# A fused graph-and-scan kernel: the first group's u projections one body sooner, and the B and C projection one step sooner

## What is computed

```
x = x + gnn(norm(x), adj)
x = x + ffn(norm(x))

gnn:  e = leaky_relu(sj + si + ab);  a = adj * exp(e);  transition = a / (rowsum(a) + 1e-12)
      H = sum over k of (Xk @ Wk[k] + bk[k]),  Xk = transition @ Xk;   relu(H)

ffn:  h = x @ W_fc1.T + b_fc1
      u, z = split(h @ W_in.T);  u = silu(causal convolution of u over 4 taps + conv_b)
      dt, B, C = split(u @ W_xproj.T)               # 32 + 16 + 16 columns
      delta = softplus(dt @ W_dt.T + b_dt)
      state[t] = exp(delta * A) * state[t-1] + (delta * u) * B[t]     # 1024 channels x 16 states
      y = sum over states of state * C + u * D;  y = y * silu(z)
      out = (y @ W_out.T) @ W_fc2.T + b_fc2
```

## Time and profile before

| | |
|---|---|
| median of 3 runs | 3723.85 us (3723.45 to 3725.98) |
| the profiled execution | 3726.6 us, its span 3724.8 us |
| instructions in the span | 43683 |
| DVE busy | 3520.6 us (95%) |
| PE busy, its weight loads | 3459.2 us (93%), 1949.2 us (52%) |
| POOL busy | 3411.5 us (92%) |
| ACT busy | 2961.1 us (79%) |
| mean granted TensorE clock | 0.988 of full speed |
| DMA | 183.68 MB, mean 49 GB/s |

### The profile page before, as it was taken

The page is one execution under the profiler, slowest core; times in us unless marked ns, Lnnn a source line. Parts: engine busy times, 40 slices in busy tenths (PEclk is TensorE's granted clock), DMA queues, the critical chain, the costliest instruction groups (busy, mean ns, idle before and its releaser), DMA issues.

```text
span 3724.8 us, 43683 instructions
## 1 busy us (share of the span) xinstructions
PE 3459.2 (93%) x11130; PEld 1949.2 (52%) x11130; DVE 3520.6 (95%) x2877; ACT 2961.1 (79%) x6578; POOL 3411.5 (92%) x1703
## 2 busy tenths in 40 slices
PE   6899999999999999999999999999999999999887
PEld 3555555555555555555555555555555555555443
DVE  0499999999999999999999999999999999999998
ACT  2588878888888888888788888888888888887774
POOL 0299999999999999999999999999999999999998
PEclk9899999999999999999999999999999999999999
DMA  3111101111101111100111110111110111110110
GB/s 112 53 56 59 59 9 53 56 58 58 59 9 53 56 59 58 58 23 39 56 58 58 59 44 18 58 56 58 58 59 9 53 56 59 58 54 9 46 51 9
DMA packets 50720, 183.68 MB, mean 49 GB/s; under 512 B 7356, under 2 KB 33220, under 8 KB 42086
## 3 DMA queue, kind: packets, MB, share of 16 engines
q1 hardware_dynamic: 48898, 174.17, 12.1%
q10 hardware_dynamic: 1636, 7.83, 0.6%
HBM read 164.15 MB, written 17.83 MB: 49 GB/s over the span
## 4 chain that ended last, share of the span: by engine, by line
POOL 56%; issue 32%; PE 5%; DVE 4%; ACT 2%; POOLq 1%; DMA 0%; SPq 0%; DVEq 0%; ACTq 0%
POOL st L425 38%; POOL st L416 10%; POOL du_sb L406 4%; POOL delta L398 3%; DVE st L967 2%; DVE st L955 1%; PE y_ps L775 1%; POOL rstd L383 1%; POOLq L192 1%; ACT dec L491 1%; PE g L926 1%; PE g L795 0%; PE dec L700 0%; DMA rows<-bk_dram 0%; PE d_ps L812 0%
## 5 line engine op out<-in xcount | busy, mean ns | idle before, releaser
L425 POOL TENSOR_TENSOR st<-st,bc 128x1024 f32<-128x1024 f32 x1024 | 2405.0, 2364 | 146.0 <-DVE st L967 146.0
L967 DVE TENSOR_TENSOR_SCAN st<-dec,st 128x1024 f32<-128x1024 f32 x1024 | 2312.6, 2274 | 23.4 <-ACT dec L491 18.5
L775 PE MATMUL y_ps<-st,ident 128*128 128x512 f32 x4096 | 1919.0, 603 | 122.6 <-POOL st L425 120.3
L491 ACT ACTIVATE dec<-delta,decay 128x254 f32<-128x254 f32 x4096 | 1691.5, 463 | 310.1 <-DVE st L967 308.1
L775 PEld LDWEIGHTS y_ps<-st,ident 128*128 128x128 f32 x4096 | 742.7, 190 | 964.9 <-issue 643.9
L955 DVE TENSOR_TENSOR st<-du,bc 128x1024 f32<-128x1024 f32 x736 | 883.8, 1201 | 22.3 <-ACT du L477 22.0
L416 POOL TENSOR_TENSOR st<-du_sb,bc 128x1024 f32<-128x1024 f32 x288 | 680.8, 2364 | 0.1
L812 PE MATMUL d_ps<-xnT,wxz 128*128 128x256 f32 x1024 | 264.5, 404 | 70.2 <-DVE u L992 69.5
L992 DVE SCALAR_TENSOR_TENSOR u<-d_ps,chan,u 128x250 f32<-128x250 f32 (+2 forms) x768 | 306.0, 465 | 7.6 <-ACT u L539 7.6
L539 ACT ACTIVATE u<-d_ps,bconv,chan 128x256 f32<-128x256 f32 x256 | 129.8, 557 | 223.7 <-PE d_ps L812 223.6
L812 PEld LDWEIGHTS d_ps<-xnT,wxz 128*128 128x128 f32 x1024 | 199.8, 200 | 158.6 <-DVE u L992 104.5
(11 more groups left out here) (111 smaller groups left out, 2513.5 us busy)
## 6 DMA issues: line engine op xcount, KB each, us to landing
bc<-bc_dram SPq DMA_DIRECT2D x64, 2048.0 KB, 9.8
xg<-x_dram SPq DMA_DIRECT2D x32, 256.0 KB, 11.5
x_dram<-xg SPq DMA_DIRECT2D x32, 256.0 KB, 2.0
last_x<-x_dram SPq DMA_DIRECT2D x32, 256.0 KB, 2.6
out_dram<-last_x SPq DMA_DIRECT2D x32, 256.0 KB, 2.1
bc<-w_inT_dram ACTq DMA_DIRECT2D x1, 4096.0 KB, 14.0
adjt<-adjT_dram SPq DMA_DIRECT2D x32, 128.0 KB, 11.2
bc<-w_out_dram ACTq DMA_DIRECT2D x1, 2048.0 KB
```

Of the source, the lines that this page charges most:

```text
L425: nc.gpsimd.tensor_tensor(st[:, sl, :, :, :], st[:, sl, :, :, :], bc[:, p, 1, SU * q:SU * q + SU, None, :].to_broadcast([P, SU, 2, T]), AL ...
L491: a = nc.scalar.activation(dec[:, v % 2, s, j, :].rearrange("p (b t) -> p b t", b=PAIR)[:, :, 1:], delta[:, p, 2 * i + j, :].rearrange("p ...
L775: mm = nc.tensor.matmul(y_all, ident[:, :], st[:, sl, s, :, :].rearrange("p j t -> p (j t)"), start=False, stop=(q == Q - 1 and s == SU - ...
L967: nc.vector.tensor_tensor_scan(h, dec[:, v % 2, :, :, :].rearrange("p s j t -> p (s j t)"), h, 0.0, ALU.mult, ALU.add).then_inc(S["scanned ...
```

## The change

It has two parts. The u projections of group 0 with their evacuation and taps, and the constants of the convolution that they need, move from body -1 (steps -1 to 7) to body -2 (steps 16 to 26); the other groups keep their places. And the two halves of the dt/B/C projection move from steps 12 and 13 to steps 11 and 12 on PE in all bodies, while ACT's copy of their result stays in step 14.

```diff
-X_STEPS = (12, 13)
+U_OF_0, U_READY_OF_0 = (16, 19, 22, 25), (17, 20, 23, 26)
+X_STEPS, X_READY = (11, 12), 14
...
             def body(act, k, p, scan, dense, ends, begins):
                 r = 1 - p
                 for v in range(U):
-                    if dense and v in U_READY:
+                    if ends and not scan and not dense and v in U_READY_OF_0:
+                        evacuate_u(act, 0, p, U_READY_OF_0.index(v))
+                    if dense and scan and v in U_READY:
                         evacuate_u(act, k + 1, r, U_READY.index(v))
...
-                if v - 1 == X_STEPS[1]:
+                if v == X_READY:
                     wait(act, "proj_mm", g + 1)
...
                     if dense:
-                        dense_pe(pe, k + 1, r, v, ends)
-                    if ends and v + 1 == U:
+                        dense_pe(pe, k + 1, r, v, ends, scan)
+                    if ends and not dense and v in U_OF_0:
+                        u_of_0(pe, p, U_OF_0.index(v))
+                    if ends and dense and v + 1 == U:
                         first_u(pe, k + 2, p)
...
+            def u_of_0(pe, r, i):
+                if i == 0:
+                    first_u(pe, 0, r)
+                else:
+                    wait(pe, "taps", 6 * i)
+                    project_u(pe, 0, r, i)
+
+            def dense_pe(pe, g, r, v, ends, scan):
+                if scan and v in U_STEPS:
...
-            def conv(dve, g, r, v):
-
-                if v in U_READY:
-                    for n in range(6):
-                        tap(dve, g, r, U_READY.index(v), n)
+            def conv(dve, g, r, i):
+
+                for n in range(6):
+                    tap(dve, g, r, i, n)
...
                     dve.wait_ge(S["bias_row"], 2)
-                    dve.wait_ge(S["w_dense"], 16 * len(DENSE_LOADS))
-                    conv_constants(dve)
...
-                    if dense:
-                        conv(dve, k + 1, r, v)
+                    if dense and scan and v in U_READY:
+                        conv(dve, k + 1, r, U_READY.index(v))
+                    if ends and not scan and not dense:
+                        if v == U_OF_0[0]:
+                            dve.wait_ge(S["w_dense"], 16 * len(DENSE_LOADS))
+                            conv_constants(dve)
+                        if v in U_READY_OF_0:
+                            conv(dve, 0, p, U_READY_OF_0.index(v))
```

More of the change, by code:

```diff
@@ L814, in project_u @@
                 mm.then_inc(S["u_mm"], 1)
-            def dense_pe(pe, g, r, v, ends):
-                if v in U_STEPS:
+            def u_of_0(pe, r, i):
[6 more added lines that the diff above has]
+                if scan and v in U_STEPS:
                     i = U_STEPS.index(v)
```

## The result

The changed kernel takes 3734.89 us (median of 10 executions, 3731.41 to 3740.29), the kernel before 3726.22 us on the same chip (10 executions, 3723.45 to 3729.82). The ratio is 1.0025, 95% interval 1.0017 to 1.0033: slower by a quarter of a per cent, and 2.4 us above the upper end of the predicted range. The forecast of 3724.8 stood on a median of three executions of the kernel before; with ten that median is 2.4 us higher. So of the 10.1 us between forecast and measurement 2.4 are the baseline, and the rest is the effect of the change, +8.7 where +0.9 was forecast. The profiled execution of the changed kernel is the longest of its ten, 3740.29 us with a span of 3738.5; its span is 13.7 us longer than that of before, where the medians differ by 8.7.

A forecast was written before the change was run, and what follows sets the result against it. A ring through DVE, POOL and PE bounds each body, with 0.14 us slack at the gate. Terms +3.9 - 2 - 1 = +0.9 us on the median 3723.85 gave 3724.8 us, range 3717.5 to 3732.5.

The forecast's parts named there:

- the falls of TensorE's clock in the bodies: Rival, 10 in 100: PE stretches at 1.2 GHz recur in bodies, 0.9 us a body; with 12 bodies, 3736 us.
- the first part's +3.9: Prologue: u of group 0 in body -2 loses 10.0 us ahead of att, saves 6.1 behind it; +0.6 to +7.5.
- The ring: Body: gate of step 18, DVE to scan, POOL, PE to unit 15's sum, gate, without a pause; period 110.95 us.
- The hand-over of 0.04: Gate of step 18: where it really waits for PE, it starts 0.04 us behind the modelled end of the sum.
- The last bodies: The last, longest DVE wait for du, 2.6 us, where PE has fewer matmuls: counted -1 us (0 to -1.5).
- the DVE gets all its waits back: Rival, 12 in 100: the DVE's du and decay waits in the bodies are all saved, 33 us; time 3695 us.
- the term +10.0: Body -2: att ends at 107.0 instead of 97.00, a mix of full and low clock; +6.7 to +13.6 us.
- -6.1: Body -1: from att to the SiLU of u, time saved as PE loses four projections, in us.
- The ping-pong at full clock: Body -2: four pairs of 5.56 us each take 22.2 us from xnT's end; att ends at 103.7.
- The sum for the low clock: Body -2 at 1.2 GHz: a pair takes 6.75 us, a projection 3.18, and att ends at 110.6.
- -3: Second part: B and C a step sooner, -2 us over 30 bodies and -1 us at the last du wait.

The follow-up runs named there:

- the fill: Changed kernel plus two zero-weight matmuls (512 and 256 columns) on PE ahead of the third u projection in each full body: 3728.24 us, ratio 1.0006 to the kernel before.
- the first part alone: Kernel before plus only u of group 0 moved to body -2, B and C left in steps 12 and 13: 3731.53 us, ratio 1.0018.
- both fills: Changed kernel plus seven unread matmuls in body -2 and two zero-weight matmuls ahead of the third u projection in full bodies: 3725.58 us, ratio 0.9999.
- fills that keep PE at work: Changed kernel plus seven unread 512-column matmuls on PE in body -2: 3732.84 us, ratio 1.0019 to the kernel before.
- the gate alone moved: Kernel before with only the gate of step 18 put behind its scan on the DVE: 3763.17 us, ratio 1.0100.
- the copy moved too: Kernel before plus B and C in steps 11 and 12, and the gate of step 18 behind its scan on the DVE: 3720.14 us, ratio 0.9987.

## Why the prediction was wrong

One step failed: the forecast put the falls of TensorE's clock in the bodies at almost nothing. A second term, the first part's +3.9, came out at +5.3, within its own range. The ring held.

**The ring: right.** The forecast had PE, not the DVE, at the end of the ring, a gate waiting about 1.0 us and a period of 110.88; the trace has 0.9 to 1.2 (0.5 behind each of the six waits ahead of taps) and 110.87. The hand-over of 0.04 from the earlier trace rows holds in the bodies. The last bodies give back 1.2 us where 1 was counted. With the falls taken away the bodies gain 4.1 us, 2.8 without the one long fall of before (forecast: 3).

**The rival "the DVE gets all its waits back": wrong, as judged.** The Trainium skill's page "Perfetto Trace Analysis", section "Identifying the Most-Contended Engine", judges TensorE's headroom by its weight loads' share (here 52%) and its use of peak FLOP/s, and not by matmul busy time. The trace does not bear out the reading that such an engine holds nothing up: the gate starts 0.04 behind PE's sum in a usual body.

**The clock in the bodies: the step that failed.** The forecast put it to one side: "Once in 30 it is in the sum already; from 8 bodies on it decides", at "0.9 a body", with 10 in 100. The profiled execution had six such bodies; three cost 1.1 each, about the price named, and three 2.8: 11.8 us in all, less the 1.3 that before paid in its one. That this execution is the longest of its ten is part of the size; the medians of the runs with and without the fill are 8.7 and 3.0 above before, 5.7 apart. The price was taken from the one row that before had the earlier trace rows, a fall with a wait of 1.58; those with 10 us at 1.2 GHz had no row. The warning sign was in view: each third projection of the trace follows some 2.0 us of idle PE, and so each body is exposed. The fill ahead of that projection removes all six late bodies and leaves the usual period at 110.89, so the cause is shown. The sign that the prediction named for this rival, waits for `u` ahead of taps, is what the trace has. Why a period that is 0.08 us shorter meets the longer falls is not shown. Each of the two prices comes back every eight bodies, and the kernel with the first part alone, at the old period, had one of 1.58 like before. This fits the sentence "A body that is a little shorter meets the clock's changes elsewhere", but no run varied the period by itself.

**The first part: the mechanism right, the term +10.0 between what two executions show.** From `att` to SiLU the forecast had -6.1, measured -5.8 (28.17 against 33.97). The ping-pong at full clock, 22.7 from `xnT` to `att`, was measured as 22.55. The end of `att` came 11.35 later, 11.2 counted from the end of `xnT`: two projections ran at 1.2 GHz in part (3.09, 2.92) and the fourth in full (3.78), with part of the hop. In the run of the first part alone it came 9.6 later by the same count. The sum for the low clock was itself short: it took 3.18 for a projection at 1.2 GHz, which was one in part; one in full takes 3.78. From the SiLU to gate 1 a further 1.1 us is lost (104.68 against 103.54), which the sum did not have; a stretch at a low clock is longer there (0.67 from 140 to 160 us; before, 0.66 to 150 and 0.83 to 160), and no run isolates this. Gate 1 is +6.7 in the profiled execution of the changed kernel and +3.2 in that of the part alone, whose median is +5.3; forecast +3.9, range to +7.5. The Trainium skill's "TensorE: Matmul & The Clock Gate", section "What's actually happening", says that the throttled clock is the default and that activity releases it. The trace agrees in kind: fills that keep PE at work take 4.7 us off. The upper end to which the prediction led this was not reached: +9.6 and +11.2 of 6.7 to 13.6, a mix of the two clocks as forecast.

**The sum.** Forecast +3.9 - 3 = +0.9. Shown: +5.3 for the first part, +1.0 for the second where -3 stood, 8.7 together in the medians of another run; the 2.4 between is inside what the intervals allow. With both fills it is -0.7; that fills help the old order too has to be kept in mind here.

## What to carry to other kernels

Look for every wait of PE of about 2 us in a steady loop, and ask what runs right behind it and how much slack that has: the clock may fall there, for 3 or for 10 us, and the price is set by the place as much as by the length: here the shortest falls cost nothing at the third u projection, where there is slack, and 1.1 to 1.4 us each on the ring; at that projection those of 10 us cost 2.8. A change that wins a tenth of a microsecond a body by shifting waits can lose more by the clock. A few matmuls that nobody needs, put into the idle time of PE off the path, are a cheap remedy and a sharp experiment at once. Compare such a fill with the old order filled as well, or the fill's gain is taken for the change's. And where two ways meet at one wait, take both away together: with the gate alone moved a body without a fall still took 110.97 (and the falls made the kernel slower by 1%), with the copy moved too it took 110.22.

## What the runs showed of the hardware

- Behind 2.0 us of idle PE in an otherwise full body the granted clock can fall to 1.2 GHz, but need not: with the gate behind its scan the same idle time is followed by a third projection of 1.99 in every body. In the changed kernel, with 1.45 us of it filled (0.72 left) the granted clock stays at 1.00 over the bodies. Matmuls with all-zero weights keep the clock up as well.
- At the third projection the falls come in 14 bodies of the changed kernel, nearly every second one, and in 9 before; their length differs: one projection at 3.45, or 10 us at 0.51.
- PE can be busier and the kernel faster: with the fill ahead of the third projection 3092.5 us against 3079.1 in the same stretch, 11.1 us sooner over 30 bodies.
- One pair of the ping-pong takes 5.56 us at full clock, and a projection of eight matmuls 1.99 us at 2.4 GHz and 3.78 us at 1.2 GHz.
- The first 80 us of executions of kernels with the same beginning differ by up to 3 us (the end of `xnT` at 78.1 to 81.1, without a fill ahead of it).
